# Closing up the first twelve steps of the expert stage: gate and up ahead of the next transposes, the down product one step sooner

## What is computed

```python
logits = xt @ Wg.T + bg
top_vals, top_idx = jax.lax.top_k(logits, 2)
rw = jax.nn.softmax(top_vals, axis=-1)
gu = jnp.einsum('th,ehf->tef', xt, Wgu) + bgu[None]
gate = jnp.minimum(gu[..., ::2], 7.0)
up = jnp.clip(gu[..., 1::2], -7.0, 7.0)
glu = gate * jax.nn.sigmoid(gate * 1.702)
out_e = jnp.einsum('tef,efh->teh', (up + 1.0) * glu, Wd) + bd[None]
out = jnp.einsum('teh,te->th', out_e, cw)          # cw: the two weights of each token
x = x + out
```

## Time and profile before

| | us |
|---|---|
| median of 3 runs | 623.36 (623.08 to 624.58) |
| the profiled execution | 623.25 |
| its span in the trace | 621.5 |
| expert stage, first transposes to last weighing | 481.05 to 590.3 |
| first send to last send on POOL | 492.21 to 598.06 |
| reading back, adding, writing out | 599.4 to the end |
| share of the span that PE, DVE, ACT, POOL are busy | 86%, 86%, 79%, 72% |

### The profile page before, as it was taken

The page is one execution under the profiler, slowest core; times in us unless marked ns, Lnnn a source line. Parts: engine busy times, 40 slices in busy tenths (PEclk is TensorE's granted clock), DMA queues, the critical chain, the costliest instruction groups (busy, mean ns, idle before and its releaser), DMA issues.

```text
span 621.5 us, 20543 instructions
## 1 busy us (share of the span) xinstructions
PE 536.7 (86%) x6805; PEld 454.2 (73%) x6806; DVE 535.3 (86%) x1528; ACT 490.9 (79%) x1423; POOL 446.0 (72%) x555
## 2 busy tenths in 40 slices
PE   0689999999999999999999999999846989898900
PEld 0357989888898988988899989898742666666600
DVE  4789999999999999999999999999965777777606
ACT  0469999999999999999999999999842666666600
POOL 7174856789898898988889888877254277777730
PEclk9989999999999999999999999999975999999955
DMA  9699231229307295632931751377011343333139
GB/s 260 181 314 318 37 71 27 45 54 314 85 21 203 54 314 136 242 69 54 311 86 20 233 170 44 95 284 144 10 29 47 87 114 95 101 80 89 46 102 304
DMA packets 70980, 82.14 MB, mean 132 GB/s; under 512 B 8372, under 2 KB 48844, under 8 KB 70884
## 3 DMA queue, kind: packets, MB, share of 16 engines
q1 hardware_dynamic: 57268, 68.13, 38.3%
q0 software_dynamic: 4608, 8.47, 4.2%
q10 hardware_dynamic: 9008, 4.30, 2.5%
HBM read 19.35 MB, written 46.84 MB: 106 GB/s over the span
## 4 chain that ended last, share of the span: by engine, by line
PE 73%; DVE 8%; issue 5%; DMA 5%; ACT 4%; POOL 2%; SPq 1%; ACTq 1%; POOLq 0%; DVEq 0%
PE bank L1159 17%; PE bank L1160 16%; PE bank L1161 16%; PE bank L1255 8%; PE bank L1305 5%; PE bank L1330 3%; DMA ctx_sb<-results 2%; PE bank L1338 2%; DMA ctx_sb<-in_ctx_dram 2%; PE bank L1387 2%; PE bank L1365 1%; PE bank L1169 1%; PE bank L1285 1%; ACT probs L527 1%; POOL places L700 1%
## 5 line engine op out<-in xcount | busy, mean ns | idle before, releaser
L527 ACT ACTIVATE probs<-bank,nbias 128x128 f32<-128x128 f32 x512 | 146.4, 369 | 4.1
L757 POOL DMA_INDIRECT results<-z,stage x80 | 80.3, 1003 | 41.5 <-ACT z L572 23.8
L1002 DVE TENSOR_TENSOR pT<-bank,pT 128x512 f16<-128x512 f32 x128 | 87.3, 682 | 6.5 <-ACT pT L539 5.2
L981 DVE TENSOR_REDUCE qmax<-bank 128x4 f32<-128x512 f32 x128 | 87.0, 680 | 0.0
L1161 PE MATMUL bank<-keys,q_pad 128*128 128x128 f16 x480 | 86.6, 219 | 0.0
L1160 PE MATMUL bank<-keys,q_pad 128*128 128x128 f16 x480 | 86.6, 219 | 0.0
L1159 PE MATMUL bank<-keys,q_pad 128*128 128x128 f16 x480 | 86.6, 219 | 0.0
L539 ACT ACTIVATE pT<-bank 128x512 f16<-128x512 f32 x128 | 78.3, 612 | 4.0 <-PE bank L1255 4.0
L1255 PE MATMUL bank<-ident,probs 128*128 128x128 f32 x512 | 79.2, 278 | 2.2 <-DVE pT L1002 2.1
L700 POOL DMA_INDIRECT places<-payload,slots x64 | 65.4, 1022 | 16.4 <-issue 12.3
L1159 PE MATMUL bank<-xT,w_qkv 128*128 128x256 f16 x256 | 71.7, 280 | 2.6 <-DVE xT L821 1.7
(11 more groups left out here) (220 smaller groups left out, 2007.9 us busy)
## 6 DMA issues: line engine op xcount, KB each, us to landing
places<-z SPq DMA_DIRECT2D x8, 4160.0 KB
q_pad<-q_nat SPq DMA_DIRECT2D x120, 128.0 KB, 2.4
stage<-places SPq DMA_DIRECT2D x80, 65.0 KB
ctx_sb<-results SPq DMA_DIRECT2D x14, 256.0 KB, 4.8
ctx_sb<-in_ctx_dram ACTq DMA_DIRECT2D x4, 512.0 KB, 10.6
stage<-in_L_ffn_Wgu_dram SPq DMA_DIRECT2D x1, 2048.0 KB, 8.8
out_dram<-x_sb ACTq DMA_DIRECT2D x7, 256.0 KB, 5.9
stage<-in_L_xattn_W_qkv_dram SPq DMA_DIRECT2D x3, 512.0 KB, 6.8
```

Of the source, the lines that this page charges most:

```text
L527: last = nc.scalar.activation(probs[:, b, k, :], score_bank[b][:, k * P:(k + 1) * P], ACT.Exp, bias=nbias[:, b, k:k + 1], scale=exp_scale)
L757: nc.gpsimd.indirect_dma_start(out=results, out_offset=bass.IndirectOffsetOnAxis(ap=to, axis=0), in_=z[:, (u - 5) % NZ, t, :], in_offset=None,
L981: nc.vector.tensor_reduce(qmax[:, r % 2, :], score_bank[r % 2][:, :].rearrange("p (h k) -> p h k", h=4), AX.X, ALU.max).then_inc(s["qmax_o ...
L1002: nc.vector.tensor_tensor(pT[:, r % 2, LO, :], pt_bank[:, :], pT[:, r % 2, HI, :], ALU.subtract).then_inc(s["pt_lo"], 1)
```

## The change

```diff
+        SKIP = NBUF - 2
-        def over_blocks(eng, body):
+        def over_blocks(eng, body, opening=None):
             for q in range(NBUF):
-                body(q, q, 0)
+                (opening or body)(q, q, 0)
...
+            def first_steps(q, u, i):                      # ACT
+                turned(q, u)
+                if q >= 1:
+                    sigmoids(q - 1, u - 1)
+                if q >= 3 and q != SKIP:
+                    weigh(q - 3 - (q > SKIP), u - 3 - (q > SKIP), i)
+                if 2 <= q < NBUF - 1:
+                    hidden_high(q - 2, u - 2)
+
             def expert_steps(q, u, i):
-                if block_live(q, 5):
-                    wait(act, "d_mm", q - 4)
-                    wait_sent(act, q, u, i, 5 + NZ)
...
+                if block_live(q, 4):
+                    weigh(q - 4, u - 4, i)
...
+            def first_steps(q, u, i):                      # DVE
+                if q >= 1:
+                    gate_and_up(q - 1, u - 1)
+                if 1 <= q < NBUF - 1:
+                    gated(q - 1, u - 1)
+                if 2 <= q < NBUF - 1:
+                    hidden_low(q - 2, u - 2)
...
+            def first_steps(q, u, i):                      # PE
+                if q >= 1:
+                    gate_up(q - 1, u - 1, i)
+                turn(q, u, i)
+                if q < 2:
+                    fill(ht_bank[0], 3 - q)
+                load_experts(u, i)
+                if q >= 3 and q != SKIP:
+                    down(q - 3 - (q > SKIP), u - 3 - (q > SKIP), i)
+                if 2 <= q < NBUF - 1:
+                    turn_hidden(q - 2, u - 2)
...
-                    if isinstance(q, int) and q < 4:
-                        fill(ht_bank[0], (3, 1, 2, 2)[q])
```

More of the change, by code:

```diff
@@ L565, in _, with turned @@
             nc.scalar.activation(spare[:, :], zeros[:, 0:1], ACT.Sigmoid)
-            def expert_steps(q, u, i):
-                if block_live(q, 5):
-                    wait(act, "d_mm", q - 4)
-                    wait_sent(act, q, u, i, 5 + NZ)
-                    for t in range(2):
-                        nc.scalar.activation(z[:, (u - 5) % NZ, t, :], d_bank[(u + 1) % 2][:, t * P:(t + 1) * P], ACT.Copy,
-                                             scale=rows_in[:, (u + NBUF - 5) % NBUF, t, P:P + 1]).then_inc(s["z_ok"], 1)
+            def turned(v, u):
+                wait(act, "t_mm", v + 1)
+                wait(act, "gu_mm", v - 1)
+                nc.scalar.activation(bT[:, u % 2].rearrange("p a b c -> p (a b c)"), t_bank[u % 2][:, 0:512],
+                                     ACT.Copy).then_inc(s["t_ok"], 1)
@@ new lines, in sigmoids, with hidden_high, weigh @@
+            def sigmoids(v, u):
+                wait(act, "gate_ok", v + 1)
+                wait(act, "glu_ok", v - 1)
+                nc.scalar.activation(sig[:, u % 2], gate[:, u % 2], ACT.Sigmoid, scale=ALPHA).then_inc(s["sig_ok"], 1)
+            def hidden_high(v, u):
+                wait(act, "ht_mm", v + 1)
+                wait(act, "d_mm", v - 1)
+                nc.scalar.activation(hT[:, u % 2, HI, :], ht_bank[u % 2][:, 0:256], ACT.Copy).then_inc(s["ht_hi"], 1)
+            def weigh(v, u, i):
+                wait(act, "d_mm", v + 1)
+                wait_sent(act, v, u, i, NZ)
+                for t in range(2):
+                    nc.scalar.activation(z[:, u % NZ, t, :], d_bank[u % 2][:, t * P:(t + 1) * P], ACT.Copy,
+                                         scale=rows_in[:, u % NBUF, t, P:P + 1]).then_inc(s["z_ok"], 1)
@@ L577, in expert_steps @@
[L577 to L578 removed]
+                    turned(q, u)
                 if block_live(q, 3):
[L580 to L582 removed]
+                    hidden_high(q - 3, u - 3)
@@ L583, in expert_steps @@
                 if block_live(q, 1):
[L584 to L588, removed]
+                    sigmoids(q - 1, u - 1)
+                if block_live(q, 4):
+                    weigh(q - 4, u - 4, i)
+            over_blocks(act, expert_steps, first_steps)
             for g, (first, n) in enumerate(LAST_GROUPS):
@@ L1120, in _, with gate_and_up @@
             gate_up_low(7)
+            def gate_and_up(v, u):
+                wait(dve, "gu_mm", v + 1)
+                wait(dve, "h_ok", v - 1)
+                b = u % 2
+                bank = gu_bank[b][:, :].rearrange("p (t c f) -> p t c f", t=2, c=2)
+                nc.vector.tensor_scalar(gate[:, b], bank[:, :, 0, :], scale_from[:, 5:6], LIMIT, ALU.mult, ALU.min).then_inc(s["gate_ok"], 1)
+                nc.vector.tensor_scalar(up[:, b], bank[:, :, 1, :], scale_from[:, 5:6], 1.0 + LIMIT, ALU.mult, ALU.min).then_inc(s["up_ok"], 1)
@@ new lines, in gated @@
+            def gated(v, u):
+                wait(dve, "sig_ok", v + 1)
+                wait(dve, "h_ok", v)
+                nc.vector.tensor_tensor(glu[:, :, :], gate[:, u % 2], sig[:, u % 2], ALU.mult).then_inc(s["glu_ok"], 1)
+                wait(dve, "glu_ok", v + 1)
+                wait(dve, "ht_mm", v - 1)
+                nc.vector.scalar_tensor_tensor(out=hidden[:, u % 2], in0=up[:, u % 2], scalar=1.0 - LIMIT,
+                                               in1=glu[:, :, :], op0=ALU.max, op1=ALU.mult).then_inc(s["h_ok"], 1)
@@ new lines, in hidden_low @@
+            def hidden_low(v, u):
+                wait(dve, "ht_hi", v + 1)
+                nc.vector.tensor_tensor(hT[:, u % 2, LO, :], ht_bank[u % 2][:, 0:256], hT[:, u % 2, HI, :],
+                                        ALU.subtract).then_inc(s["ht_lo"], 1)
+            def first_steps(q, u, i):
[5 more added lines that the diff above has]
+                    hidden_low(q - 2, u - 2)
@@ L1122, in expert_steps @@
             def expert_steps(q, u, i):
                 if block_live(q, 2):
[L1124 to L1130, removed]
@@ L1131, in expert_steps @@
-                if block_live(q, 1):
[L1132 to L1137, removed]
+                    gated(q - 2, u - 2)
@@ L1138, in expert_steps @@
+                if block_live(q, 1):
+                    gate_and_up(q - 1, u - 1)
                 if block_live(q, 3):
[L1139 to L1143, removed]
+                    hidden_low(q - 3, u - 3)
+            over_blocks(dve, expert_steps, first_steps)
@@ L1352, in experts_of, with turn, gate_up, turn_hidden @@
                 return known[g][at:at + 2]
+            def turn(v, u, i):
+                pe.wait_ge(block_in[u], i * 32 + 32)
+                wait(pe, "t_ok", v - 1)
+                for t in range(2):
+                    for h in range(2):
+                        at = (2 * t + h) * P
+                        last = nc.tensor.transpose(t_bank[u % 2][:, at:at + P], rows16[:, u, t, h * P:(h + 1) * P], ident16[:, :])
+                last.then_inc(s["t_mm"], 1)
+            def gate_up(v, u, i):
+                load_experts(u, i)
+                wait(pe, "t_ok", v + 1)
+                wait(pe, "up_ok", v - 1)
+                b = u % 2
+                fill(gu_bank[b], 1)
+                for t, e in enumerate(experts_of(u)):
+                    last = plus_bias(gu_bank[b][:, t * 256:(t + 1) * 256], bT[:, b, t, HI, :], bT[:, b, t, LO, :],
+                                     w_gu[:, HI, e, :], w_gu[:, LO, e, :], bias_gu[:, e, :])
+                last.then_inc(s["gu_mm"], 1)
+            def turn_hidden(v, u):
+                wait(pe, "h_ok", v + 1)
+                wait(pe, "ht_lo", v - 1)
+                for t in range(2):
+                    last = nc.tensor.transpose(ht_bank[u % 2][:, t * P:(t + 1) * P], hidden[:, u % 2, t, :], ident[:, :])
+                last.then_inc(s["ht_mm"], 1)
+            def down(v, u, i):
+                load_experts(u, i)
+                wait(pe, "ht_lo", v + 1)
+                wait(pe, "z_ok", v * 2 - 2)
+                b = u % 2
+                fill(d_bank[b], 1)
+                for t, e in enumerate(experts_of(u)):
+                    last = plus_bias(d_bank[b][:, t * P:(t + 1) * P], hT[:, b, HI, t * P:(t + 1) * P], hT[:, b, LO, t * P:(t + 1) * P],
+                                     w_d[:, HI, e, :], w_d[:, LO, e, :], bias_d[:, e, :])
+                last.then_inc(s["d_mm"], 1)
+            def first_steps(q, u, i):
[4 more added lines that the diff above has]
+                    fill(ht_bank[0], 3 - q)
+                load_experts(u, i)
+                if q >= 3 and q != SKIP:
+                    down(q - 3 - (q > SKIP), u - 3 - (q > SKIP), i)
+                if 2 <= q < NBUF - 1:
+                    turn_hidden(q - 2, u - 2)
             def expert_steps(q, u, i):
@@ L1383, in expert_steps @@
                 if block_live(q, 3):
[L1384 to L1388, removed]
-                if block_live(q, 4):
[L1390 to L1399, removed]
+                    turn_hidden(q - 3, u - 3)
+                if block_live(q, 4):
+                    down(q - 4, u - 4, i)
+            over_blocks(pe, expert_steps, first_steps)
```

2 lines of the change are left out of this document (removed).

## The result

The changed kernel takes 624.75 us (median of 22 runs) against 622.8 for the kernel before in the same series (22 runs): a ratio of 1.0033, 95% interval 1.0022 to 1.0043, so 2.0 us slower. The time on record, 624.1, was 0.65 short of it, and the time lies in the range given (622.1 to 625.7). Part of that closeness is luck: the forecast was a rise of 0.8, the rise was 2.0, and in this series the kernel before came out 0.56 lower than the 623.36 beside which the forecast was worked out. By its ratio the change just counts as slower by over 0.3%, which had 0.14; by the 625.1 that the prediction wrote for this bound it still counts as the same.

A forecast was written before the change was run, and what follows sets the result against it. PE's arrival at step 12 was taken to bound the end through pair 22. Early gains, chain waits, loads and the step 10 wait put step 12 0.8 us later: 623.25 + 0.8 = 624.1 us, range 622.1 to 625.7.

The forecast's parts named there:

- slower by over 0.3%: Whole kernel: a time above 625.1 us, given a chance of 0.14.
- What bounds the stage: Expert stage: PE's arrival at step 12 sets pair 22 and the end, one for one; 0.8 us later.
- the first send decides: Expert stage, rival: the end moves with POOL's start, 1.9 us sooner, 621.3 us; chance 0.06.
- a shift of PE: Loop entry, transposes of step 12: PE's lateness there goes through pair 22 to the end one for one.
- Gate/up ahead of the transposes: First steps: gate/up 0 starts 0.7 us sooner; each later gate/up follows by 2.15 us, waiting where the step is shorter.
- The wait for bT in step 10: Step 10, which has no down product: PE waits 0.6 us before gate/up 10.
- Down product one step sooner: First steps: first send at 490.3 instead of 492.2, but PE waits 0.1 us in each full step, 4 to 9.
- The two chains: Full steps: dependency chains between engines of 2.29 and 2.28 us a step, against PE's own 2.19.
- the down product itself: PE's steps: a down product was taken to last 0.66 us.
- small hitches within a product, 0.1 a step: Upper bound of the range: PE's hitches within a product may add 0.6 us in all.
- Loads: Expert-number loads in steps 5, 8 and a fourth in 11: 0.51 us each, less 0.1 for two; bounds nothing and 0.73.
- The clock: Steps 1 and 2, rival: PE's clock falls to half for 4 us, adding some 2 us, 626.1 us.

The follow-up runs named there:

- entry_late: The kernel before with five more fills ahead of gate/up 10 in step 11; ratio 1.0001 of the kernel before.
- turn_first_2: The changed kernel with the four transposes of a step ahead of gate/up again in the first twelve steps; ratio 1.0016 of the kernel before.
- lean_before_2: The kernel before without the fill ahead of each down product (40 fills); ratio 0.9996 of the kernel before.
- lean_short_2: The changed kernel with the new order in the first six steps alone and no fills ahead of down products; ratio 0.9994 of the kernel before.

## Why the prediction was right, and where its sizes were off

*What bounds the stage.* Right, and shown: with the first send 1.8 sooner the last came 2.2 later, as step 12 did, with the first send 2.6 later the last came 0.25 later, and three kernels moved both step 12 and the last send by the same 0.6 to 1.4. The rival "the first send decides" is out. But "a shift of PE" was one word too short. entry_late showed that array time is not what is shifted. Two readings ahead of it were off, too. The 3.8 us between 593.3 and 597.08 were put down to POOL being held up; waits beyond 0.30 make 1.7 of them, sends longer than 0.98 the other 2.0. And not 10 of 12 pairs reach POOL sooner but seven, which is why it stood before pair 7, where no wait was forecast.

*Gate/up ahead of the transposes.* Gate/up 0 came 0.8 sooner (0.7 said), gate/up 1 and 2 at s+3.46 and 5.63 (3.35 and 5.55 said, if 481.05 is taken off). The wait for bT in step 10 was 0.65 (0.6 said). turn_first_2 prices the whole part: 0.64 at step 12.

*Down product one step sooner.* First send at s+9.37 (9.25 said). The waits ahead of the down products were 0.13, 0.08, 0, 0.07 and 0.04 in the steps without a load (0.1 said). The two chains are there, and they cost little.

*The term that was mis-sized: the down product itself.* I took 0.66 from the one at 489.86, the fastest of the kernel before. In the changed kernel the first seven took 0.81, 0.82, 0.86, 0.81, 0.82, 0.87 and 0.98, together 1.35 over 7 x 0.66, and the last one 0.2; the hidden transposes behind them add 0.2 (0.25 for 0.22). These 1.75 us are the miss of 1.5 (29.63 against 28.1 for step 12) and a little more. The prediction had it among the bounds, "small hitches within a product, 0.1 a step", and did not ask where they come from. The earlier trace rows alone could not tell; the rows of steps 6 to 8 before, where down products of 0.73 to 0.75 stand, should have been in the sum.

*Loads.* Those of steps 5 and 8 showed as 0.40 and 0.43, where the kernel before has 0.40 and 0.50 (0.51 said, less 0.1); the fourth showed as 0.47, worth 0.6 with what follows. The Trainium skill's rule (page "TensorE: Matmul & The Clock Gate", section on the array's architectural detail: a queue of 64 instructions on TensorE) fits the gap, which did not grow to 0.73 behind the shorter transposes, though a stream that is hardly ahead of the array would give the same. entry_late says more: the 1.08 us by which the array lagged at the entry are its last 13 matmuls (two of gate/up, two transposes, a fill and eight of the down product), so some 13 must have been queued when the stream went on to the loop. That is an estimate, and it is more than "a few" and within 64; the 64 itself no run here shows.

*The sum of the 2.33 us at step 12.* By the runs, 0.64 is the order of gate/up and transposes with its wait for bT, and 0.61 the fourth load; 1.1 is left. The timeline has it so, against the kernel before: eight down products 1.2 longer (6.8 against 5.65, each to the next instruction; the 1.75 above was counted from the prediction's 0.66), the wait for bT 0.65, loads 0.4, waits ahead of the down products 0.2, hidden transposes 0.1, and 0.2 back in gate/up and at the start of down 0. The timed 2.0 us and the 2.2 us in the profiles agree.

*The clock.* 1.00 from the first transposes to the last down product; the rival is out, in lean_before_2 and lean_short_2 too, with 40 fills fewer.

What stays open: why the stream is slow just in the down products. Their weights are addressed through registers, as gate/up's are, and a matmul of 128 columns keeps the array for only 0.055; lean_before_2 suggests that each such matmul takes the stream some 0.07 to 0.095 (0.53 to 0.76 for eight), but no kernel with fixed weight addresses was run. Nor was it tried whether PE's waits as such take its lead away; that the slow products stand right behind a wait or a load is seen, and in the loop it isn't the only cause: in step 13 of the kernel before the eight matmuls take 0.79 too, behind hidden transposes that waited for nothing.

## What to carry to other kernels

Ask of a gap on PE whether the array waits for data or for its instructions: put a fill ahead of it, and if the end does not move, the array's work was not the path and neither is the work you plan to save there. A stage moved one step sooner is worth nothing if its consumer waits again later on; find the last wait of the consumer first. And where the start of a stage varies by 2 us between executions, count from the stage's own first instruction: single profiles of the changed order then agreed within 0.01 us at step 4, those of the order before within 0.25, where 31 runs don't tell 0.6.

## What the runs showed of the hardware that was not expected

- Five fills of 512 columns (1.08 us) ahead of the loop's entry cost under 0.1; the entry's gap went from 0.97 to 0. Eight fills ahead of down products cost 0.7 of their 1.7; eight taken away gave back 0.3 to 0.4.
- Eight matmuls of 128 columns with register addresses take 0.45 at best and 0.53 to 0.76 where no fill keeps the array busy ahead of them (lean_before_2, first twelve steps).
- The start of the expert stage varied between 479.4 and 481.9 us over ten profiles of kernels with the same code ahead of it.
- POOL's indirect sends take 0.98 us, but some 1.1 to 1.25; summed over 80 sends the excess was between 1.1 and 2.7 us from one execution to the next.
